# Four PSUM banks for the relation products of a fused graph network kernel, the attribute maximum in the gates' bank, and a constant row brought by a transfer

## Chip, cores and metric

The kernel runs on one core of one Trainium2 chip. The metric is the device time of one execution in microseconds (us). The engines are TensorE (PE; its weight loads are listed apart as PEld), VectorE (DVE), ScalarE (ACT), GpSimd (POOL, called Pool here) and SyncE (SP, which issues transfers). The results of TensorE go to PSUM, which has eight banks of 512 fp32 columns on each of 128 partitions.

## What is computed

A graph with 1250 nodes of 512 features and 20000 edges goes through four layers, each with a residual sum and a layer norm:

```
x = layernorm(x + segment_sum(edge_weight * (x @ W0)[src], dst) + b0)
# the relation layer is applied twice inside the second step (h = relu(first))
def rgcn_gate_layer(x, ...):
    w = einsum('rb,bio->rio', att, basis)            # 2 relations out of 30 bases
    msgs[r] = sigmoid(x_j @ gate_w[r]) * x_j @ w[r]
    return segment_sum(msg of the edge's relation, row) + x @ root + bias
x = layernorm(x + rgcn(relu(rgcn(x))))
x = layernorm(x + gcn(x))                            # weights deg^-1/2, self loop
x = layernorm(x + attention(x, att_bias = edge_attr))  # 8 heads, softmax over a node's edges
```

The attention bias of an edge is `edge_attr_8`; the row maximum of the logits is subtracted before `exp`.

## The kernel before

Nodes are cut into NT = 10 tiles of 128 rows. Neighbour sums are dense products with counting matrices (CT for the two relations) held in SBUF, built at the start. Every fp32 operand is split into a high and a low fp16 part, and a product is the three terms of `THREE` (high x high, low x high, high x low). The order of work on each engine is written out by hand, with semaphores between engines; there is no planner.

**Relation stages.** `z_tile(s, k)` on PE (L1856 to L1873) makes for node tile k the products of x with the mixed weights: in stage s = 1 and 2 (the two relation layers) two products a tile, one per relation, each 12 matmuls of 512 columns (L1872); in stage 3 (the graph convolution) one product with a bias term. Product number `zi` counts through all stages and goes to bank `zi % 2`. `z_high` (ScalarE, L1504) copies it, scaled by the sigmoid gate, to the high half of Z; `z_low` (VectorE, L1042) subtracts to get the low half and raises `zl_made`. PE may reuse a bank when `zl_made` has reached `zi - 1`.

**Beside them on VectorE in layer 1**, after the subtractions of tile 5: the maximum of the edge attributes (L1069) and the low half of root1 (`split_low(0)`, L1017, 2048 columns). PE then turns the maxima into a row (L1943, bank 7, after tile 6), VectorE reduces it (L1083), PE spreads it over 125 partitions (L1946, bank 6, after tile 8) and VectorE subtracts it from all attributes (L1088, `bdiff_made`). ScalarE takes the exponential (L1526). In layer 2 VectorE does `split_low(1)` after tile 5. The gates of layer 2 open on ScalarE in two calls (`gates_opened`, L1494).

**After layer 1's products** PE waits for `bdiff_made` (L2015) and does `roots(0)` to `roots(3)` (L1992, 12 matmuls of 384 columns each, banks 4 to 7), then `chunk_sums` (L2008), with the weight mixes of layer 2 between them (`mix`, L1727, fp32). Each mixed weight is copied by ScalarE (L1467), subtracted by VectorE (L1010, inside `matched`) and stored to DRAM in pairs from ScalarE's queue (`mix_stored`, L1402); the buffers of two pairs alternate. The basis blocks (1 MB each) are loaded by SP (L633): the third and fourth of layer 2 when the last product of layer 1 has ended, each later one when a mix has ended. Gate sums of layer 2 (`gates(1, i)`, L1852) use bank 3, the first of them in the sixth chunk. Between the first loads and layer 1, Pool zeroes the bias array in DRAM by 160 transfers (L807, L810).

**Pool's scatter.** From layer 1's end on, Pool adds the edge values into the bias array by 160 indirect transfers (L844), two at a time, 8 to each of 20 batches. Before the last batch it waits for `loops_out` and writes the constant 64 into the row KH[64] of 10240 fp16 elements (L839), which the attention scores need (`kone_made`, waited for before `scores(0)`).

**Up to the scores.** VectorE computes 80 row maxima (`row_max`, L1223). SP, in its order, copies the heads (L737 to L740), sends the first row of maxima, loads Wo, waits for all scatters, issues two bias loads (L752) and only then sends the second row of maxima (L745), which PE waits for before its third group of scores (L2215). VectorE multiplies with the bias in L1260.

Of the kernel before, what the change touches and what calls it, by code (L numbers as in the profile page):

```python
# [13 lines left out]
P = 128  # L14
# [50 lines left out]
def gnn_resnorm(nc, a, out):  # L65
    ctx = ExitStack()
    with ctx:
# [234 lines left out]
        negative = r2[0:DK, o2 + NN // 2 + P:o2 + NN // 2 + P + DK // 2].bitcast(F16)  # L302
        yT = XX[:, NT * D:NT * D + FT * RB].rearrange("p (f n) -> p f n", f=FT)
# [136 lines left out]
        kone_made = sem("kone_made")  # L440
        wo_in = sem("wo_in")
# [115 lines left out]
        def GATHERED(b):  # L557

            return 0 if b < NT else 2

# [49 lines left out]
        def _(sp):  # L610
# [143 lines left out]

            for o_ in range(FT):
                heads_copied(o_)
# [23 lines left out]
        def _(pool):  # L780
# [49 lines left out]
            for n in range(ZE + ZB + 2 * ZA, ZF):  # L830
                zeros(n)
            pool.iota(bramp, [[-1, GC * EC]], base=GC * EC, channel_multiplier=0,
                      allow_small_or_imprecise_dtypes=True).then_inc(bramp_made, 1)

            pool.wait_ge(zero_out, 16 * ZF)
            for b in range(BATCHES):
                if b == BATCHES - 1:
                    pool.wait_ge(loops_out, NT)
                    pool.memset(KH[DK:DK + 1, :, :], MSCALE).then_inc(kone_made, 1)  # L839
# [13 lines left out]
        def _(dve):  # L853
# [182 lines left out]
            def z_low(s, k):  # L1036

                for r in range(ZRELS[s]):
# [3 lines left out]
                    V.scalar_tensor_tensor(Z[:, r, 1, k, :], mm_out(zi % 2, D), scale, Z[:, r, 0, k, :], ALU.mult,  # L1042
# [13 lines left out]
            for k in range(1, NT):  # L1056
# [24 lines left out]
                if k == 7:  # L1081
                    dve.wait_ge(bmt_done, 1)
                    step(V.tensor_reduce(bmax1[0:HEADS, :], mm_out(7, EC, HEADS), AX.X, ALU.max))  # L1083
                    V.tensor_scalar(diag8[0:HEADS, :], ident[0:HEADS, 0:HEADS], bmax1[0:HEADS, :], None,
                                    ALU.mult).then_inc(bdiag_made, 1)
                if k == 9:
                    dve.wait_ge(bmb_done, 1)
                    V.tensor_tensor(attr[0:EC, :, :], attr[0:EC, :, :],  # L1088
                                    PS[0:EC, 6, 0:HEADS].rearrange("p (u h) -> p u h", u=1).broadcast_to(
# [284 lines left out]
        def _(act):  # L1374
# [123 lines left out]
            def z_high(s, k):  # L1498

                for r in range(ZRELS[s]):  # L1500
# [3 lines left out]
                    S.activation(Z[:, r, 0, k, :], mm_out(zi % 2, D), ACT.Copy, scale=scale).then_inc(zh_made, 1)  # L1504
# [204 lines left out]
        def _(pe):  # L1709
# [130 lines left out]
            def gates(layer, i):  # L1840
# [5 lines left out]
                if i == 0 and layer:  # L1846
                    pe.wait_ge(gate_made, 2)
                if i == ZBATCH:
                    pe.wait_ge(gate_made, 2 * layer + 1)
# [6 lines left out]
            def z_tile(s, k):  # L1856
# [5 lines left out]
                for r in range(ZRELS[s]):  # L1862
                    zi = Z0[s] + k * ZRELS[s] + r
                    if zi >= 2:
                        pe.wait_ge(zl_made, zi - 1)
# [5 lines left out]
                    for n, (lhs, rhs) in enumerate(terms):  # L1871
                        ins = T.matmul(mm_out(zi % 2, D), lhs, rhs, start=n == 0, stop=n == len(terms) - 1)  # L1872
# [66 lines left out]
            for k in range(2, NT):  # L1939
                z_tile(1, k)  # L1940
                if k == 6:
                    pe.wait_ge(bmax_made, 1)
                    T.transpose(mm_out(7, EC, HEADS), bmax[0:EC, :], ident[0:EC, 0:EC]).then_inc(bmt_done, 1)  # L1943
                if k == 8:
                    pe.wait_ge(bdiag_made, 1)
                    T.matmul(mm_out(6, HEADS, EC), ones[0:HEADS, 0:EC], diag8[0:HEADS, :], start=True,  # L1946
# [37 lines left out]
            def roots(c):  # L1984
# [3 lines left out]
                if p_:  # L1988
                    pe.wait_ge(h_made, c - FT + 1)
                for n, (p, q) in enumerate(THREE):  # L1990
# [24 lines left out]
            pe.wait_ge(bdiff_made, 1)  # L2015
# [347 lines left out]
```

## Time and profile before

| | |
|---|---|
| median of 3 runs | 1230.68 us (1227.04 to 1235.55) |
| profiled execution | 1232.0 us |
| its span, first to last instruction | 1230.2 us |
| PE busy | 1167.2 us (95%) |
| DVE busy | 847.2 us (69%) |
| ACT busy | 442.4 us (36%) |
| POOL busy | 374.1 us (30%) |
| mean granted TensorE clock | 0.984 |

A busy PE is not a PE at full speed: the granted clock is 1.00 or about half of it, and a row's busy time grows where it is low. All places are given in us from the span's start. In a timeline row the number in brackets is the idle time of that engine just before the row, with what ended it.

### The profile page before, as it was taken

How to read it: one execution, taken by the hardware profiler on the slowest of the kernel's cores; microseconds unless marked ns; L12 is line 12 of the kernel's file. 1: busy time of each engine (PE TensorE's matmuls, PEld its weight loads, DVE VectorE, ACT ScalarE, POOL GpSimd, SP SyncE). 2: the span in 40 equal slices, each digit the busy share in tenths (PEclk: the TensorE clock that was granted, in tenths of full speed). 3: DMA queues.
4: the chain of work that ended last, by engine and by line, in shares of the span. 5: the costliest groups of instructions: out<-in, count | busy, mean ns of one | idle time of the engine just before them, and what ended most of it. 6: DMA issues, size and time to landing. Idle time of an engine off the chain costs nothing.

```text
span 1230.2 us, 21619 instructions
## 1 busy us (share of the span) xinstructions
PE 1167.2 (95%) x8077; PEld 539.9 (44%) x8078; DVE 847.2 (69%) x1333; ACT 442.4 (36%) x600; POOL 374.1 (30%) x340
## 2 busy tenths in 40 slices
PE   6989999999999989999999999999999899999997
PEld 2334444333444433364444444454333465555553
DVE  7577777344442655652378884657999799899897
ACT  1456666322232222212301103135552355445354
POOL 3034441000350224445554564555557100000000
PEclk9999999999999999999999999999999899999999
DMA  9669995987987988661122212113323566565652
GB/s 311 237 200 326 326 331 150 358 350 261 329 283 272 312 316 286 227 210 2 2 40 47 36 19 70 3 2 45 35 34 58 184 232 228 200 221 198 202 186 111
DMA packets 67490, 222.74 MB, mean 181 GB/s; under 512 B 33200, under 2 KB 38064, under 8 KB 50140
## 3 DMA queue, kind: packets, MB, share of 16 engines
q1 hardware_dynamic: 34846, 156.38, 36.0%
q0 software_dynamic: 28208, 53.10, 18.0%
q10 hardware_dynamic: 4350, 12.07, 2.8%
q8 instruction: 60, 0.98, 0.3%
q14 instruction: 26, 0.21, 0.1%
HBM read 199.90 MB, written 59.92 MB: 211 GB/s over the span
## 4 chain that ended last, share of the span: by engine, by line
PE 45%; DVE 11%; issue 6%; DMA 4%; ACT 2%; ACTq 0%; DVEq 0%
PE PS L1920 13%; PE PS L1872 6%; PE PS L2228 4%; PE PS L2008 4%; PE PS L2215 4%; DVE R L1223 4%; DVE R L1260 4%; DMA w_d<-R 3%; PE PS L2097 2%; PE PS L2274 2%; PE PS L1992 2%; PE PS L1727 2%; PE PS L2245 1%; DVE R L1297 1%; PE PS L1837 1%
## 5 line engine op out<-in xcount | busy, mean ns | idle before, releaser
L844 POOL DMA_INDIRECT bias_d<-R x160 | 276.6, 1729 | 310.2 <-DMA bias_d<-R 204.8
L1920 PE MATMUL PS<-R 128*128 128x512 f16 x900 | 206.3, 382 | 0.0
L810 POOL DMA_DIRECT2D bias_d<-bias_d x159 | 82.6, 526 | 267.3 <-PE PS L1920 123.1
L1683 ACT ACTIVATE R<-PS 128x1024 f32<-128x1024 f32 (+1 forms) x100 | 106.3, 1088 | 108.7 <-PE PS L2215 78.6
L1872 PE MATMUL PS<-W,XX 128*128 128x512 f16 x600 | 137.7, 389 | 5.5 <-DVE R L1042 4.6
L1920 PEld LDWEIGHTS PS<-R 128*128 128x128 f16 x900 | 84.3, 98 | 118.7 <-issue 27.6
L1797 PE MATMUL PS<-R,XX 125*128 125x512 f16 (+2 forms) x612 | 123.1, 343 | 5.7 <-DVE R L958 4.4
L1223 DVE CUSTOM_DVE_ANT_0 R<-PS,R 128x1250 f16<-128x1250 f32 x80 | 116.8, 1460 | 5.5 <-PE PS L2151 2.9
L958 DVE TENSOR_SCALAR R<-W 125x1250 f16<-125x1250 f16 x160 | 89.6, 604 | 37.8 <-PE PS L1797 35.4
L2228 PE MATMUL PS<-R 128*32 128x256 f32 (+1 forms) x1600 | 101.4, 388 | 5.2 <-DVE R L1260 5.2
L2215 PE MATMUL PS<-R 128*128 128x256 f16 (+3 forms) x800 | 100.5, 276 | 5.3 <-ACT R L1683 2.1
L1042 DVE SCALAR_TENSOR_TENSOR R<-PS,gate,R 128x512 f16<-128x512 f32 x50 | 37.3, 750 | 91.8 <-ACT R L1504 91.8
L1260 DVE SCALAR_TENSOR_TENSOR R<-R,W 128x512 f32<-128x512 f32 (+1 forms) x136 | 85.9, 674 | 16.6 <-ACT R L1683 14.2
L1872 PEld LDWEIGHTS PS<-W,XX 128*128 128x128 f16 x600 | 58.7, 100 | 78.6 <-issue 14.1
L2008 PE MATMUL PS<-R 128*128 128x384 f16 (+2 forms) x480 | 92.2, 340 | 0.0
L2215 PEld LDWEIGHTS PS<-R 128*128 128x128 f16 (+1 forms) x800 | 75.1, 99 | 36.8 <-issue 20.2
L1797 PEld LDWEIGHTS PS<-R,XX 125*128 x612 | 56.6, 98 | 65.7 <-issue 23.2
L1487 ACT ACTIVATE stat<-stat 128x1 f32<-128x1 f32 x30 | 8.8, 295 | 181.4 <-DVE stat L1030 165.9
L2008 PEld LDWEIGHTS PS<-R 128*128 128x128 f16 x480 | 44.0, 98 | 58.3 <-issue 28.3
L1504 ACT ACTIVATE R<-PS,gate 128x512 f16<-128x512 f32 x50 | 34.3, 687 | 96.8 <-PE PS L1872 96.1
L2228 PEld LDWEIGHTS PS<-R 128*32 128x32 f32 x1600 | 44.7, 108 | 48.0 <-DVE R L1260 13.5
L2097 PE MATMUL PS<-XX,W 128*128 128x512 f16 (+1 forms) x288 | 61.3, 345 | 1.1 <-ACT R L1622 1.1
(242 smaller groups left out, 1470.3 us busy)
## 6 DMA issues: line engine op xcount, KB each, us to landing
bias_d<-bias_d POOLq DMA_DIRECT2D x159, 320.0 KB, 5.4
R<-in_basis_s SPq DMA_DIRECT2D x32, 1024.0 KB, 7.2
W<-in_basis_s SPq DMA_DIRECT2D x28, 1024.0 KB, 6.3
W<-bias_d SPq DMA_DIRECT2D x27, 1024.0 KB, 4.9
XX<-bias_d SPq DMA_DIRECT2D x13, 1024.0 KB, 4.9
R<-key_d SPq DMA_DIRECT2D x20, 500.0 KB
R<-R SPq DMA_DIRECT2D x120, 80.0 KB, 4.9
W<-bias_d SPq DMA_DIRECT2D x7, 904.0 KB, 4.6
```

The source lines that it names most:

```text
L844: pool.indirect_dma_start(bias_d, bass.IndirectOffsetOnAxis(ap=idx[:, c:c + 1], axis=0), attr[:, c, :], None, bounds_check=DUMP + GC * P - ...
L958: V.tensor_scalar(hot[0:EC, FIXED * (j % 2) + m, 0:NODES], iota16[0:EC, 0:NODES], base[0:EC, bass.ds(t4, 1), j], key[0:EC, bass.ds(lo + m, ...
L1223: V.tensor_tensor_reduce(out=junk[:, 0:NODES], in0=PS[:, b0:b0 + 3, :].rearrange("p a b -> p (a b)")[:, 0:NODES], in1=nmask[:, i, 0:NODES] ...
L1260: ins = V.scalar_tensor_tensor(p, p, BIG, b, ALU.min, ALU.mult)
L1683: S.activation(ER[n % 4][:, :, 0:w, :].rearrange("p g r u -> p g u r"), PS[:, 2 * (n % 2):2 * (n % 2) + 2, :].rearrange("p a (e r) -> p a ...
L1797: ins = T.matmul(mm_out(3 * (j % 2) + b, p1 - p0), own[0:EC, bass.ds(c, 1), :, :].rearrange("p c m w -> p (c m w)"), hots(p0, p1), start=f ...
L1872: ins = T.matmul(mm_out(zi % 2, D), lhs, rhs, start=n == 0, stop=n == len(terms) - 1)
L1920: ins = T.matmul(mm_out(SUM_BANK(s, i), D), lhs, rhs, start=n == 0, stop=n == len(terms) - 1)
L2008: ins = T.matmul(mm_out(4 + f, hi - lo), lhs, rhs, start=False, stop=n == len(terms) - 1, skip_group_check=True)
L2097: ins = T.matmul(mm_out(BANK_OF("q", g), hi - lo), W16[:, 1 + which, q, f, o_ * P:(o_ + 1) * P], XT16[:, p, f, lo:hi], start=n == 0 and f ...
L2215: ins = T.matmul(PS[:, 2 * (n % 2) + i // 2, (i % 2) * RB:(i % 2) * RB + w], key[:, h, j * P:(j + 1) * P], query[:, h, cols], start=k == 0 ...
L2228: ins = T.matmul(PS[32 * i:32 * i + 32, 4 + q, e * RB:e * RB + w], VA[:, j, 4 * q + i, 32 * e:32 * e + 32], ER[n % 4][:, i // 2, 0:w, i % ...
```

## The change

Products of stages 1 and 2 rotate over banks 0, 1, 6 and 7 (`ZBANK`; the third and fourth product of stage 1 go to banks 4 and 5), so PE waits for the subtraction of four products back instead of two. Stage 3 keeps banks 0 and 1. Two waits are added where 6 and 7 come into use, and `roots(2)` and `roots(3)` wait for the last two subtractions of layer 1. The two small matmuls of the attribute maximum go to free columns of bank 3, and PE's wait for `bdiff_made` moves from before `roots(0)` to before the first gate of layer 2. Pool fills a block of 128 x 80 values early, and SP sends it to the row KH[64] ahead of the head copies; Pool's memset and wait before the last batch go.

```
+        scale_row = r2[:, o2 + NN // 2 + P + DK // 2:o2 + NN // 2 + P + DK // 2 + HEADS * NN // P // 2].bitcast(F16)
...
+        def ZBANK(s, k, r):
+
+            m = k * ZRELS[s] + r
+            if s == 3:
+                return m % 2
+            return 2 + m if s == 1 and m in (2, 3) else (0, 1, 6, 7)[m % 4]
...
+            sp.wait_ge(scale_row_made, 1)
+            sp.wait_ge(loops_out, NT)
+            sp.dma_start(KH[DK:DK + 1, :, :].rearrange("u h (k n) -> u (h k) n", n=HEADS * NN // P),
+                         scale_row).then_inc(kone_made, 16)
             for o_ in range(FT):
                 heads_copied(o_)
...
+            pool.memset(scale_row, MSCALE).then_inc(scale_row_made, 1)
...
             for b in range(BATCHES):
-                if b == BATCHES - 1:
-                    pool.wait_ge(loops_out, NT)
-                    pool.memset(KH[DK:DK + 1, :, :], MSCALE).then_inc(kone_made, 1)
...
-                    V.scalar_tensor_tensor(Z[:, r, 1, k, :], mm_out(zi % 2, D), scale, Z[:, r, 0, k, :], ALU.mult,
+                    V.scalar_tensor_tensor(Z[:, r, 1, k, :], mm_out(ZBANK(s, k, r), D), scale, Z[:, r, 0, k, :], ALU.mult,
...
-                    step(V.tensor_reduce(bmax1[0:HEADS, :], mm_out(7, EC, HEADS), AX.X, ALU.max))
+                    step(V.tensor_reduce(bmax1[0:HEADS, :], PS[0:HEADS, 3, P:P + EC], AX.X, ALU.max))
...
-                                    PS[0:EC, 6, 0:HEADS].rearrange("p (u h) -> p u h", u=1).broadcast_to(
+                                    PS[0:EC, 3, DK:DK + HEADS].rearrange("p (u h) -> p u h", u=1).broadcast_to(
...
-                    S.activation(Z[:, r, 0, k, :], mm_out(zi % 2, D), ACT.Copy, scale=scale).then_inc(zh_made, 1)
+                    S.activation(Z[:, r, 0, k, :], mm_out(ZBANK(s, k, r), D), ACT.Copy, scale=scale).then_inc(zh_made, 1)
...
                 if i == 0 and layer:
                     pe.wait_ge(gate_made, 2)
+                    pe.wait_ge(bdiff_made, 1)
...
-                    if zi >= 2:
-                        pe.wait_ge(zl_made, zi - 1)
+                    held = 2 if s == 3 else 4
+                    if s == 3 or zi - Z0[s] >= held:
+                        pe.wait_ge(zl_made, zi - held + 1)
+                    if (s, k, r) == (1, 3, 0):
+                        pe.wait_ge(xt_made, NT)
+                    if (s, k, r) == (2, 1, 0):
+                        pe.wait_ge(h_made, CHUNKS)
...
-                        ins = T.matmul(mm_out(zi % 2, D), lhs, rhs, start=n == 0, stop=n == len(terms) - 1)
+                        ins = T.matmul(mm_out(ZBANK(s, k, r), D), lhs, rhs, start=n == 0, stop=n == len(terms) - 1)
...
-                    T.transpose(mm_out(7, EC, HEADS), bmax[0:EC, :], ident[0:EC, 0:EC]).then_inc(bmt_done, 1)
+                    T.transpose(PS[0:HEADS, 3, P:P + EC], bmax[0:EC, :], ident[0:EC, 0:EC]).then_inc(bmt_done, 1)
...
                 if p_:
                     pe.wait_ge(h_made, c - FT + 1)
+                elif f >= 2:
+                    pe.wait_ge(zl_made, Z0[1] + RELS * NT - FT + f + 1)
...
             pe.wait_ge(w16_made, 1)
-            pe.wait_ge(bdiff_made, 1)
             for c in range(FT):
                 roots(c)
...
-            pe.wait_ge(kone_made, 1)
+            pe.wait_ge(kone_made, 16)
```

On PE, at the end of layer 1's products, this stood before (L1946 spreads the maximum, L1872 are the last two products, L1992 the roots, L2008 the first chunk sum):

```order
L1946 MATMUL PS<-R,ones 125x8 [waits bdiag_made]
L1872 MATMUL PS<-W,XX 128x512 [waits zl_made,xt_made]
L1872 MATMUL PS<-W,XX 128x512 x11
L1872 MATMUL PS<-W,XX 128x512 [waits zl_made]
L1872 MATMUL PS<-W,XX 128x512 x11
L1992 MATMUL PS<-XX,W 128x384 [waits bdiff_made,w16_made]
```

In the changed kernel the same place on PE reads so, with lines 17 to 20 higher:

```order
L1964 MATMUL PS<-R,ones 125x8 [waits bdiag_made]
L1890 MATMUL PS<-W,XX 128x512 [waits zl_made,xt_made]
L1890 MATMUL PS<-W,XX 128x512 x11
L1890 MATMUL PS<-W,XX 128x512 [waits zl_made]
L1890 MATMUL PS<-W,XX 128x512 x11
L2012 MATMUL PS<-XX,W 128x384 [waits w16_made]
L2012 MATMUL PS<-XX,W 128x384 x23
L2012 MATMUL PS<-XX,W 128x384 [waits zl_made]
L2012 MATMUL PS<-XX,W 128x384 x11
L2012 MATMUL PS<-XX,W 128x384 [waits zl_made]
```

No matmul moved; the wait for the attribute subtraction left the first root, and the third and fourth root got one each for a relation product's subtraction.

On SP, before the head copies (L673 loads weights, L737 to L740 copy heads), this stood before:

```order
L704 DMA R<-key_d 128x1000 [waits bm_made] x10
L673 DMA R<-in_Wk 128x2048 [waits bsum_done]
L673 DMA R<-in_Wv 128x2048
L737 DMA R<-R 64x2560 [waits qkh_made]
L739 DMA R<-R 64x2560 [waits qkh_made]
```

And now, on SP, with the new transfer at L767:

```order
L714 DMA R<-key_d 128x1000 [waits bm_made] x10
L683 DMA R<-in_Wk 128x2048 [waits bsum_done]
L683 DMA R<-in_Wv 128x2048
L767 DMA R<-R 1x128x80 [waits loops_out,scale_row_made]
L747 DMA R<-R 64x2560 [waits qkh_made]
L749 DMA R<-R 64x2560 [waits qkh_made]
```

The transfer of the key row was put ahead of all head copies.

## Rows read from the trace of the kernel before

**Rows 1.** The page, part 4: share of the last-ending chain by engine.
```profile
PE 45%; DVE 11%; issue 6%; DMA 4%; ACT 2%; ACTq 0%; DVEq 0%
```
**Rows 2.** Waits of PE: who for whom, us in total, times, longest.
```profile
PE PS L1872 <- DVE R L1042: 4.6, 3, 2.3
PE PS L1992 <- DVE R L1088: 3.0, 1, 3.0
```
**Rows 3.** Timeline of PE, 339 to 399: start, us, instruction, count, idle before.
```profile
339.60 26.06 PE L1872 MATMUL PS<-W,XX 128*128 128x512 f16 x120
365.49 0.27 PE L1943 MATMUL PS<-ident,R 125*8 125x125 f32 x1
368.05 12.20 PE L1872 MATMUL PS<-W,XX 128*128 128x512 f16 x48 [2.28 <-DVE R L1042]
380.17 0.38 PE L1946 MATMUL PS<-R,ones 8*125 8x8 f32 x2
380.49 5.35 PE L1872 MATMUL PS<-W,XX 128*128 128x512 f16 x24
388.89 9.45 PE L1992 MATMUL PS<-XX,W 128*128 128x384 f16 x48 [3.05 <-DVE R L1088]
398.18 1.46 PE L2008 MATMUL PS<-R 128*128 128x384 f16 x8
```
**Rows 4.** Timeline of DVE, 361 to 369.
```profile
361.90 2.46 DVE L1069 TENSOR_REDUCE R<-R 125x8 f32<-125x1280 f32 x1
...
364.94 2.29 DVE L1017 TENSOR_TENSOR W<-R,W 128x2048 f16<-128x2048 f32 x1
367.15 1.40 DVE L1042 SCALAR_TENSOR_TENSOR R<-PS,gate,R 128x512 f16<-128x512 f32 x2
```
**Rows 5.** Windows: length, busy PE, PEld, DVE, ACT, POOL, PE clock, DMA share, GB/s.
```profile
368.00:370.00 2.00, 1.95 (x5) 0.73 (x6) 0.56 (x1) 0.00 (x0) 0.00 (x0) 0.51 1.13 319
...
395.00:398.00 3.00, 3.00 (x20) 1.79 (x19) 0.00 (x0) 0.00 (x0) 0.00 (x0) 1.00 0.07 23
```
**Rows 6.** Timeline of PE, 559 to 612 (layer 2's products).
```profile
559.83 0.44 PE L1852 MATMUL PS<-gw,XX 128*128 128x2 f16 x12
562.14 7.03 PE L1872 MATMUL PS<-W,XX 128*128 128x512 f16 x24 [1.87 <-DVE R L1042]
569.00 0.74 PE L1852 MATMUL PS<-gw,XX 128*128 128x2 f16 x24
569.61 26.06 PE L1872 MATMUL PS<-W,XX 128*128 128x512 f16 x120
596.15 15.70 PE L1872 MATMUL PS<-W,XX 128*128 128x512 f16 x72 [0.47 <-DVE R L1042]
```
**Rows 7.** Timeline of ACT at 560.
```profile
560.52 1.27 ACT L1504 ACTIVATE R<-PS,gate 128x512 f16<-128x512 f32 x2
```
**Rows 8.** Chain and timeline of PE at the end of layer 2's mixes.
```profile
445.49 8.37 DMA w_d<-R
...
458.21 5.30 PE L1992 MATMUL PS<-XX,W 128*128 128x512 f16 x12 [1.33 <-ACT R L1535]
```
**Rows 9.** Timeline of POOL: a scatter after layer 1, and those around the memset.
```profile
494.33 3.52 POOL L844 DMA_INDIRECT bias_d<-R  x1 [8.24 <-DVE R L1136]
...
929.28 1.55 POOL L844 DMA_INDIRECT bias_d<-R  x1 [2.15 <-DMA bias_d<-R]
...
932.72 8.63 POOL L839 MEMSET R<- 1x10240 f16 x1
941.51 1.56 POOL L844 DMA_INDIRECT bias_d<-R  x1 [0.17 <-issue]
...
947.05 1.55 POOL L844 DMA_INDIRECT bias_d<-R  x1 [2.12 <-DMA bias_d<-R]
```
**Rows 10.** Timeline of SP's queue before the scores: issues of transfers.
```profile
963.10 0.81 SPq L752 DMA_DIRECT2D W<-bias_d  x2
967.51 0.77 SPq L745 DMA_DIRECT2D R<-R  x1
```

More of the change, by code:

```diff
@@ L302, in gnn_resnorm @@
         negative = r2[0:DK, o2 + NN // 2 + P:o2 + NN // 2 + P + DK // 2].bitcast(F16)
+        scale_row = r2[:, o2 + NN // 2 + P + DK // 2:o2 + NN // 2 + P + DK // 2 + HEADS * NN // P // 2].bitcast(F16)
+        assert o2 + NN // 2 + P + DK // 2 + HEADS * NN // P // 2 <= KEPT
         yT = XX[:, NT * D:NT * D + FT * RB].rearrange("p (f n) -> p f n", f=FT)
@@ L440, in gnn_resnorm @@
         kone_made = sem("kone_made")
+        scale_row_made = sem("scale_row_made")
         wo_in = sem("wo_in")
@@ L1942, in _ @@
                     pe.wait_ge(bmax_made, 1)
-                    T.transpose(mm_out(7, EC, HEADS), bmax[0:EC, :], ident[0:EC, 0:EC]).then_inc(bmt_done, 1)
+                    T.transpose(PS[0:HEADS, 3, P:P + EC], bmax[0:EC, :], ident[0:EC, 0:EC]).then_inc(bmt_done, 1)
                 if k == 8:
                     pe.wait_ge(bdiag_made, 1)
-                    T.matmul(mm_out(6, HEADS, EC), ones[0:HEADS, 0:EC], diag8[0:HEADS, :], start=True,
+                    T.matmul(PS[0:EC, 3, DK:DK + HEADS], ones[0:HEADS, 0:EC], diag8[0:HEADS, :], start=True,
                              stop=True).then_inc(bmb_done, 1)
```

## Prediction

> **What bounds the kernel now.** I read the page's chain first: TensorE carries 45% of the chain that ended last, VectorE 11% [rows 1]. So a microsecond counts only where PE stands still or runs slow. Next comes the list of waits for PE alone, of which I kept the rows whose line the change touches: the relation products (L1872) wait for VectorE 3 times, 4.6 us in all, and the root products (L1992) once, 3.0 us, for the attribute subtraction of L1088 [rows 2]. PE's timeline gives the places: 2.28 us idle before 368.05 and 3.05 before 388.89 in layer 1 [rows 3], 1.87 before 562.14 and 0.47 before 596.15 in layer 2 [rows 6]. Last, VectorE's timeline says why it was late [rows 4], and the clock windows say what a gap costs after it ended [rows 5].
>
> A relation product is 12 matmuls of 512 columns. In steady state 120 of them start at 339.60 and the next instruction at 365.49: 25.89/120 = 0.2157 us each, 2.59 us a product [rows 3]. Its readers, a ScalarE copy and a VectorE subtraction of some 0.7 us each [rows 4, 7], take well under that, so two banks are enough while nothing else stands in VectorE's queue. The stalls are where something does.
>
> **The rotation, layer 1 (A).** Before 365.5 VectorE does the attribute maximum (2.46 us) and the split of root1 (2.29 us), and comes to the next two subtractions only at 367.15 [rows 4]. From 365.49 to 380.17 are 14.68 us, where 48 matmuls at the steady rate are 10.36 and the small transpose some 0.2: 4.1 us lost, 2.28 of them idle and 1.8 a slow start [rows 3]. The granted clock was 0.51 in the 2 us after the gap, the lower of its two levels, 1.2 GHz [rows 5]. With four banks the product that started at 368.05 needs only the subtraction four products back, the last one before the maximum of 361.90; the first product that needs one of the late subtractions would start near 370.8, and they end at 368.6 [rows 4]. All 4.1 us go. Banks 4 and 5 stand in for 6 and 7 once, for products 2 and 3, since the turned x is still there. The two added waits, on that turn and in layer 2 on the last hidden chunk, are for results that come before the products ahead of them have ended: I cost them at nothing, and at 1 us each if that cover failed.
>
> **The wait for the subtraction (B).** The last 24 product matmuls start at 380.49 and could be followed at 380.49 + 24 x 0.2157 = 385.67. The 48 root matmuls of 384 columns start at 388.89, and the chunk sums at 398.18 [rows 3]. At the steady rate scaled by columns, 0.2157 x 384/512 = 0.162 us, the roots are 7.8 us. Without the wait and the slow start the sums would begin at 393.5: 4.7 us earlier. What is late next: roots 2 and 3 use banks 6 and 7, which the last two products now hold, and wait for their subtractions. The last one ends about 1.5 us after its product (a copy and a subtraction), while roots 0 and 1 occupy PE for 3.9 us, so 2.4 us of cover are left. The moved wait stands before the first layer-2 gate, in the sixth chunk, tens of microseconds after the subtraction. The two small matmuls of the maximum cost the same in bank 3.
>
> **The rotation, layer 2 (C).** Twelve gate matmuls start at 559.83 (0.31 us to the next), then 24 product matmuls should take 5.18 us; they end at 569.00, so 9.17 - 5.49 = 3.7 us are lost, 1.87 idle and 1.8 slow [rows 6]. The wait is for VectorE behind ScalarE, whose two copies start only when the gates open, at 560.52 [rows 7]. The split of root2 costs 596.15 - 569.61 - 25.89 = 0.65 us more [rows 6]. Four banks cover both: C = 4.3 us. The third relation stage keeps two banks.
>
> **Does the gain of A and B pass on?** Behind them come the layer-2 mixes, whose stores follow one another: a buffer pair is reused when an earlier store has landed. Late in that stretch a store of 8.37 us stands in the chain, and PE starts its roots only at 458.21, 12 of them in 5.30 us, slow again [rows 8]. I expect the stretch to move as a block, for first mix, first store and basis loads are all released by PE. What does not move is the zeroing of the bias array, still in the DMA queues when two basis loads go out behind the last product. These two would be needed near 395 and 398, some 9 us sooner, and are released only 4 us sooner. Today the engines are already empty at 395 to 398, a DMA share of 0.07 [rows 5], so with the same bytes and an earlier start they should land by 394. Bounds: all 8.8 us pass on, or 3 if loads and stores hold their time; I take the full sum, since every step is released by PE or by the step before. The slow start at 458 may go, or another come: 2.6 us either way.
>
> **The key row.** Pool's memset lasts 8.63 us, and the next scatter starts at 941.51. Scatter pairs otherwise start 5.54 us apart (941.51 to 947.05), so it would have started at 929.28 + 5.54 = 934.8: the chain gets 6.7 us shorter [rows 9]. Is it on the path? The bias load behind it goes out at 963.10, the last row of maxima at 967.51 [rows 10]: Pool leads by 4.4 us, and today the memset costs nothing. But the maxima end 13.1 us earlier after the change, while Pool's chain, which keeps its own pace after the chunk sums, moves only by A + B = 8.8: without the edit its lead would be 0.1 us, and the landing of the bias loads would show. With it the lead is 4.4 + 8.8 + 6.7 - 13.1 = 6.8 us. The new transfer (128 pieces of 160 bytes) leaves SP when the loops are out, ahead of the head copies, and is needed by the first scores, over 100 us later; whether it takes 1 or 20 us is hidden. Behind its wait on SP stand the head copies, which wait for projections that PE itself begins around then. The small memset of its source runs while Pool waits for transfers. Value 0, bounds -1 and +1.
>
> **Sum.** 4.1 + 4.7 + 4.3 = 13.1 us. Against the profiled execution, 1232.0 us (span 1230.2): 1218.9. The median shown, 1230.7, would give 1217.6. I forecast 1218, own range 1214 to 1223: 5.3 of the 13.1 us are slow starts, of which another execution may have fewer. One per cent, 12.3 us, is about what a measurement of this kernel can tell from no change; the forecast is near that edge.
>
> **The rivals.**
> 1. The loads and stores eat part of A and B. For it: the chain before 458.21 runs through a store [rows 8]. Against: PE releases them. Only 3 of the 8.8 pass: 1232.0 - 3 - 4.3 = 1224.7. Chance 0.17.
> 2. Pool's scatter chain does not follow the 8.8, its pace being that of the traffic. Against: at 494.33 it had waited 8.24 us for VectorE's sums, so it is pulled along [rows 9]. Then the bias loads go out at 963.1 - 6.7 = 956.4, 2 us behind the last row of maxima (954.4). Allowing them 5 us or less to land, up to 4 are lost: 1218.9 + 4 = 1223. Chance 0.08.
> 3. VectorE is the late one, and stall A only moves to a later product. It gives back A: 1218.9 + 4.1 = 1223. Against: the 2.2 us of room between 368.6 and 370.8. Chance 0.05.
> 4. Slower: the rotation itself lowers the clock. PE would meet small gaps at each change of bank, and the clock fall for a tile. 24 matmuls took 6.86 us after such a fall (562.14 to 569.00) instead of 5.18 [rows 6]; 1.7 us on 19 tiles is 32 us: 1218.9 + 32 = 1251. From 8 tiles on it turns the sign. Against: today's two banks change just as often, and 120 matmuls run at 0.2157 us without a gap [rows 3]. Chance 0.03.
>
> The fourth has a rule beside it. The Trainium skill, "TensorE: Matmul & The Clock Gate", section "A second HAM failure mode: psum-queue depth-cycling", tells of a kernel of N=512 matmuls that cycled through banks each iteration and whose micro-idles made the clock fall again and again. By it the relation stages would lose time and the change would be slower; the steady stretch of this trace disagrees, and I side with the trace.
>
> **How the numbers follow.** Forecast 0.67, rivals 0.17, 0.08, 0.05 and 0.03. The range, 1212 to 1227, holds the first three rivals and leaves out the fourth; its low end has 2.6 us for one slow start less and some noise of the runs (1227 to 1236 before). Faster by over 1% is below 1218.4, two thirds of the forecast's share by where its centre lies: 0.45. Slower by over 1%: 0.04, rival 4 and a hundredth for the unnamed. Within 1%: 0.51.
>
> **What would show it.** PE's waits should have no row of relation products on VectorE outside stage 3, and none of roots on the attribute subtraction. From the first layer-1 steady product to the first chunk sum (58.6 us, 339.60 to 398.18) 8.8 us should go, and the clock stay at 1.00. Layer 2's products should take 4.3 us less. Pool's last scatter should lead the last row of maxima by more than 4.4 us. I am wrong if roots wait for the last subtractions, if mixes wait for their basis loads, if the store-bound stretch grows by what was gained, or if the gap before the scores grows.

## The result and the profile after

The changed kernel took 1217.81 us (median of 4 runs, 1216.62 to 1219.36), the kernel before 1230.88 us on the same chip (4 runs, 1227.04 to 1235.55). The ratio is 0.9885, 95% interval 0.9837 to 0.9932. The forecast was 1218.0 us. The profiled execution took 1217.02 us, its span was 1215.1 us and its mean granted clock 0.988 (before: 1232.0, 1230.2 and 0.984).

PE's timeline over layer 1's products in the changed kernel, against [rows 3]: start, us, instruction, count, and in brackets idle time before.

```profile
339.45 26.06 PE L1890 MATMUL PS<-W,XX 128*128 128x512 f16 x120
365.34 0.27 PE L1961 MATMUL PS<-ident,R 125*8 125x125 f32 x1
365.45 10.52 PE L1890 MATMUL PS<-W,XX 128*128 128x512 f16 x48
375.91 0.38 PE L1964 MATMUL PS<-R,ones 8*125 8x8 f32 x2
376.22 5.35 PE L1890 MATMUL PS<-W,XX 128*128 128x512 f16 x24
381.41 7.96 PE L2012 MATMUL PS<-XX,W 128*128 128x384 f16 x48
389.21 1.46 PE L2028 MATMUL PS<-R 128*128 128x384 f16 x8
```

No row has a bracket any more. The 48 matmuls after the small transpose take 10.52 us where they took 12.20, the 2.28 us ahead of them are gone, and the roots follow the last product at once. From the first product to the first chunk sum are 389.21 - 339.45 = 49.76 us; they were 58.58. The windows over the stretch where the gap was, against [rows 5]:

```profile
366.00:368.00 2.00, 2.00 (x11) 0.87 (x9) 2.00 (x3) 0.23 (x1) 0.55 (x3) 1.00 1.01 297
368.00:370.00 2.00, 2.00 (x11) 0.88 (x10) 1.17 (x2) 0.69 (x1) 0.00 (x0) 1.00 0.86 277
```

PE is busy in all of both, and the granted clock is 1.00 (2.4 GHz) where it was 0.51. VectorE (the third figure) is still at its maximum and split through the first window; only nobody waits for it. In layer 2, against [rows 6]:

```profile
542.24 5.34 PE L1890 MATMUL PS<-W,XX 128*128 128x512 f16 x24
547.42 0.44 PE L1865 MATMUL PS<-gw,XX 128*128 128x2 f16 x12
547.72 5.34 PE L1890 MATMUL PS<-W,XX 128*128 128x512 f16 x24
552.90 0.74 PE L1865 MATMUL PS<-gw,XX 128*128 128x2 f16 x24
553.51 41.60 PE L1890 MATMUL PS<-W,XX 128*128 128x512 f16 x192
```

The first 24 product matmuls behind the gates start without the 1.87 us gap and take 5.34 us instead of 7.03, and what were pieces of 120 and 72 with a 0.47 us gap is one run of 192 matmuls, at a granted clock of 1.00 (window 553.5 to 595.1). In the list of PE's waits both groups of [rows 2] are gone; of those that touch this part, these are left:

```profile
PE PS L2234 <- DMA R<-R: 3.1, 1, 3.1
PE PS L1974 <- DVE R L1130: 1.6, 2, 1.2
PE PS L2012 <- ACT R L1547: 1.0, 1, 1.0
```

The first is the scores' wait for the last row of maxima, 2.09 us in the kernel before. Around it, the last of Pool's scatters and of ScalarE's value copies, then SP's queue, against [rows 10], and PE:

```profile
944.35 1.55 POOL L856 DMA_INDIRECT bias_d<-R  x1 [0.30 <-issue]
945.54 0.60 ACT L1640 ACTIVATE R<-PS 128x512 f32<-128x512 f32 x1 [3.91 <-issue]
```
```profile
947.43 0.81 SPq L762 DMA_DIRECT2D W<-bias_d  x2
950.79 0.79 SPq L755 DMA_DIRECT2D R<-R  x1
```
```profile
955.21 3.57 PE L2234 MATMUL PS<-R 128*128 128x256 f16 x16 [3.06 <-DMA R<-R]
```

SP sends the bias loads (947.43) when every scatter has landed and the last value copy has ended, and the row of maxima (950.79) behind them. The copy ended at 945.54 + 0.60 = 946.14, so here the scatters were the last to come: the loads left 1.29 us after the copy and 3.08 us after the last scatter had started. Before, these two intervals were 0.24 and 3.00 us. "Lead" below is the time from the loads' leaving to the row's.

The page's chain by engine answers to [rows 1]:

```profile
PE 70%; DVE 11%; issue 7%; DMA 6%; ACT 5%; ACTq 0%; SPq 0%; DVEq 0%
```

PE's share rose from 45% to 70%; what had carried the rest of the chain stood elsewhere or beside PE, so I take the gain from stages, not from this line. Cut at fixed instructions, us from start to start. M runs from the first chunk sum to layer 2's products (the mixes and their stores), C from there to the first output tile, T on to the third group of scores:

| kernel | A+B | M | C | T | rest |
|---|---|---|---|---|---|
| before | 58.58 | 156.47 | 57.03 | 359.28 | 259.24 |
| after | 49.76 | 153.03 | 52.70 | 360.27 | 259.89 |

So A+B gave 8.8 us, C 4.3 us, M 3.4 us, and T and the rest took back 1.6 us. The first two are the forecast's own terms, to a tenth. The other two nobody had forecast. All stages together make this pair of traces differ by 15.0 us, where the medians differ by 13.1. The experiments had to say whether 13.1 us is what the change is worth, or what this pair of traces shows.

### The profile page after: what moved, and what is told of

The parts are those of the page before. It is cut to its first block, busy times and chain, and to the rows that moved or that the text cites. A ratio compares the mean times of both kernels' runs of the same rounds, so it can differ in the third digit from the quotient of the medians.

```text
span 1215.1 us, 21618 instructions
## 1 busy us (share of the span) xinstructions
PE 1160.9 (96%) x8077; PEld 538.1 (44%) x8078; DVE 846.8 (70%) x1333; ACT 442.3 (36%) x600; POOL 359.4 (30%) x340
## 4 chain that ended last, share of the span: by engine, by line
PE 70%; DVE 11%; issue 7%; DMA 6%; ACT 5%; ACTq 0%; SPq 0%; DVEq 0%
PE PS L1938 17%; PE PS L1890 11%; PE PS L1809 6%; PE PS L2028 5%; PE PS L2247 4%; PE PS L2234 4%; PE PS L1739 4%; DVE R L1235 4%; DVE R L1272 4%; ACT R L1461 4%; PE PS L1757 3%; PE PS L1793 2%; PE PS L2116 2%; PE PS L2293 2%; DMA w_d<-R 2%
## 5 line engine op out<-in xcount | busy, mean ns | idle before, releaser
L856 POOL DMA_INDIRECT bias_d<-R x160 | 270.9, 1693 | 308.5 <-DMA bias_d<-R 224.1
L1890 PE MATMUL PS<-W,XX 128*128 128x512 f16 x600 | 134.2, 383 | 1.2 <-DMA W<-w_d 1.2
```

The costliest lines, as they stand in the source:

```text
L856: pool.indirect_dma_start(bias_d, bass.IndirectOffsetOnAxis(ap=idx[:, c:c + 1], axis=0), attr[:, c, :], None, bounds_check=DUMP + GC * P - ...
L1890: ins = T.matmul(mm_out(ZBANK(s, k, r), D), lhs, rhs, start=n == 0, stop=n == len(terms) - 1)
```

## The experiments

The theory: the change is worth its three stalls (A 4.1, B 4.7, C 4.3 us), each an idle gap and a slow start. The rivals: M's 3.4 us belong to the change; the key row is what keeps the scores from waiting; one of the stalls was worth nothing. Each kernel ran beside the kernel before; batches had different chips, and the median of before was 1227.2 to 1232.9 us in them, so ratios carry the comparison; the 95% intervals of these ratios reach from 2 to 6 us to either side.

**The changed kernel again.** No edit.

> The changed kernel once more, nothing edited, for a tighter ratio and a second trace. Theory (the three terms 4.1 + 4.7 + 4.3 = 13.1 us): ratio near 0.9893, time 1217 to 1218.5. The first trace showed 3.3 us more than that before the second layer's products and a slow start less; if that is part of the change, the trace again has no slow start near 448 and the roots of the fifth chunk start about 9.8 us sooner than the 458.21 of before. Rival: it is chance, and the slow start shows again in some trace.

Measured: 1217.11 us (6 runs, 1212.97 to 1219.62) against 1227.18 (21 runs); ratio 0.9914, 0.9892 to 0.9935. The ratio stands for 10.6 us, with an interval of 8.0 to 13.3; the medians differ by 10.1. The profiled execution has A+B and C again at 49.76 and 52.70 us, but M at 149.68, 3.4 us less than the trace above, with the same program. Near 448 there is again no slow start (the roots of the fifth chunk start at 444.61 and 12 of them take 2.75 us), but the kernel with the memset back, below, shows one there with the same A+B (12 in 5.19 us at 447.12). So that slow start comes and goes by itself, as the rival had it.

**Two banks again**, the rest of the change left as it is. The last product then sits in the bank in which the first mix begins, so the fourth root alone waits for it.

```diff
-            m = k * ZRELS[s] + r
-            if s == 3:
-                return m % 2
-            return 2 + m if s == 1 and m in (2, 3) else (0, 1, 6, 7)[m % 4]
+            return (k * ZRELS[s] + r) % 2
...
-                    held = 2 if s == 3 else 4
-                    if s == 3 or zi - Z0[s] >= held:
-                        pe.wait_ge(zl_made, zi - held + 1)
-                    if (s, k, r) == (1, 3, 0):
-                        pe.wait_ge(xt_made, NT)
-                    if (s, k, r) == (2, 1, 0):
-                        pe.wait_ge(h_made, CHUNKS)
+                    if zi >= 2:
+                        pe.wait_ge(zl_made, zi - 1)
...
-                elif f >= 2:
-                    pe.wait_ge(zl_made, Z0[1] + RELS * NT - FT + f + 1)
+                elif f == 3:
+                    pe.wait_ge(zl_made, Z0[1] + RELS * NT)
```

> Rotation undone in both relation layers, the wait of the roots and the key row as changed. Theory: A and C come back, 4.1 + 4.3 = 8.4 us, so 1226.2 against 1217.8; PE waits 3 times for the subtraction again, 2.3, 1.9 and 0.5 us, with two slow starts. Rival (rotation is worth nothing by itself, the stall only moves): within 1.5 us of 1217.8.

Measured: 1223.78 us (8 runs), ratio 0.997, 0.9953 to 0.9986: 6.7 us behind the changed kernel where 8.4 were expected. PE's timeline of this kernel at the three places, in the fastest of the eight executions (1220.08 us), shows what can be missing:

```profile
367.46 10.52 PE L1882 MATMUL PS<-W,XX 128*128 128x512 f16 x48 [2.29 <-DVE R L1051]
...
551.52 5.34 PE L1882 MATMUL PS<-W,XX 128*128 128x512 f16 x24 [1.87 <-DVE R L1051]
...
583.84 15.70 PE L1882 MATMUL PS<-W,XX 128*128 128x512 f16 x72 [0.47 <-DVE R L1051]
```

The gaps are back to a hundredth (2.29, 1.87, 0.47 us against 2.28, 1.87, 0.47), but the work behind them runs at full rate: 10.52 us where [rows 3] has 12.20, 5.34 where [rows 6] has 7.03. A+B is 52.21 us, 2.45 over the changed kernel, and C 55.34, 2.64 over it. The gap belongs to the program; the slow start behind it comes in one execution and not in another.

**The attribute wait back before the first root.**

```diff
-                    pe.wait_ge(bdiff_made, 1)
...
+            pe.wait_ge(bdiff_made, 1)
             for c in range(FT):
                 roots(c)
```

> The wait for the attribute subtraction put back before the first root, all else as changed. Theory: B comes back, 4.7 us (3.0 idle and 1.7 slow start): 1222.5. If the store-bound stretch behind it absorbs the delay, less: within 2 us of 1217.8. If the lost slow start near 448 depends on it, up to 8 us more: 1225.8.

Measured: 1222.57 us (10 runs), ratio 0.9954, 0.9935 to 0.9973: 5.5 us behind the changed kernel. On PE:

```profile
385.44 9.47 PE L2011 MATMUL PS<-XX,W 128*128 128x384 f16 x48 [3.05 <-DVE R L1100]
```

The same 3.05 us as in [rows 3], and 9.47 - 7.96 = 1.5 us of slow start; A+B is 54.48, 4.72 us over the changed kernel. B is confirmed in place and size.

**Pool's memset back, no transfer.**

```diff
-            sp.dma_start(KH[DK:DK + 1, :, :].rearrange("u h (k n) -> u (h k) n", n=HEADS * NN // P),
-                         scale_row).then_inc(kone_made, 16)
...
-            pool.memset(scale_row, MSCALE).then_inc(scale_row_made, 1)
...
+                if b == BATCHES - 1:
+                    pool.wait_ge(loops_out, NT)
+                    pool.memset(KH[DK:DK + 1, :, :], MSCALE).then_inc(kone_made, 1)
...
-            pe.wait_ge(kone_made, 16)
+            pe.wait_ge(kone_made, 1)
```

> Pool's memset of the key row and its wait put back before the last batch, no transfer, all else as changed. Theory: Pool's chain ends 6.7 us later, so the bias loads go out at 954.1 instead of 947.4, 3.3 us behind the maxima, and the last row of maxima, which stands behind them in SP's queue, lands 3.3 to 4 us later: 1221.5, PE's wait before the scores 3.1 us growing to 6.5 or more. Rival (the memset is hidden as it was before): 1217.8.

Measured: 1217.87 us (4 runs, 1215.85 to 1222.31), ratio 0.9929, 0.9901 to 0.9956. The expected loss did not show. The timelines of POOL, ACT and SP, in order of time:

```profile
911.22 8.62 POOL L849 MEMSET R<- 1x10240 f16 x1
...
938.62 1.55 POOL L854 DMA_INDIRECT bias_d<-R  x1 [0.30 <-issue]
...
946.60 0.60 ACT L1638 ACTIVATE R<-PS 128x512 f32<-128x512 f32 x1 [3.91 <-PE PS L2146]
...
947.23 0.81 SPq L762 DMA_DIRECT2D W<-bias_d  x2
```

Pool's last scatter is out at 938.62, and yet the bias loads leave only at 947.23: 0.03 us after the end of ScalarE's last value copy (946.60 + 0.60). They wait for whichever is later, scatters or copy, and here it is the copy. From the last scatter's start to the loads are 8.61 us, where 3.0 to 3.1 us are enough when the scatters are the late ones, so this trace had some 5.6 us of cover with the memset in it. The changed kernel's first trace had none without it (944.35 and 947.43). Pool's chain simply came out earlier in this execution, and this is the only trace with one memset.

**The key row alone**, on the kernel before: only the key row's lines of the change (its block, transfer and memset; PE's wait for 16).

> The kernel before with the key row's edit alone (small memset early, transfer from SP, none on Pool before the last batch). Theory: in the traces the bias loads leave SP when both the last scatter and the last value copy are done, and these two were 0.2 us apart in the kernel before, so a shorter Pool chain gains nothing: ratio 1.00 within 0.3%. Rival: the memset was on the path, up to 6.7 us gained, ratio 0.995.

Measured: 1226.53 us (10 runs), ratio 0.9978, 0.995 to 1.0005; no difference that can be told: the interval reaches from 6 us gained to 0.6 us lost. In its trace the last scatter starts at 949.13, the last value copy ends at 957.10 and the loads leave at 957.12: the scatters had 5 us of cover and only the copy held the loads, as the theory says. The trace is also a further one of an unrotated kernel: gap A with no slow start, gaps B and C with one.

**Three banks** instead of four (0, 1 and 6).

```diff
-            return 2 + m if s == 1 and m in (2, 3) else (0, 1, 6, 7)[m % 4]
+            return 4 if s == 1 and m == 2 else (0, 1, 6)[m % 3]
...
-                    held = 2 if s == 3 else 4
+                    held = 2 if s == 3 else 3
...
-                    if (s, k, r) == (1, 3, 0):
+                    if (s, k, r) == (1, 2, 1):
...
-                    pe.wait_ge(zl_made, Z0[1] + RELS * NT - FT + f + 1)
+                    pe.wait_ge(zl_made, Z0[1] + RELS * NT - 2 * (f == 2))
```

> The changed kernel with three banks (0, 1, 6) in place of four. Theory: the product that would need one of the two late subtractions starts at about 368.2 in layer 1 and they have ended at 367.8 (first of them), in layer 2 at 562.7 against 562, so PE waits 0.3 us at most: time as changed, 1217.1 within 1.5 us, no wait of products in stages 1 and 2 above 0.5 us. Rival (the depth of four is what hides it): at least 3 us slower and a wait in the trace.

Measured: 1215.7 us (5 runs, 1210.5 to 1217.54), ratio 0.9892, 0.9842 to 0.9942. PE's rows, with no bracket at any of the three places:

```profile
361.33 10.52 PE L1890 MATMUL PS<-W,XX 128*128 128x512 f16 x48
...
542.47 5.34 PE L1890 MATMUL PS<-W,XX 128*128 128x512 f16 x24
...
548.25 41.60 PE L1890 MATMUL PS<-W,XX 128*128 128x512 f16 x192
```

The third bank does all of it; the fourth is spare.

**Four banks in layer 1 only.**

```diff
-            if s == 3:
+            if s >= 2:
                 return m % 2
...
-                    held = 2 if s == 3 else 4
-                    if s == 3 or zi - Z0[s] >= held:
+                    held = 4 if s == 1 else 2
+                    if s > 1 or zi >= held:
...
-                    if (s, k, r) == (2, 1, 0):
-                        pe.wait_ge(h_made, CHUNKS)
```

> Four banks in layer 1 only, two in layer 2. Theory: C comes back: idle 1.87 + 0.5 us always and a slow start of 1.8 us in part of the executions: 2.4 to 4.3 us more than 1217.1, so about 1220.5. The run with no rotation lost 6.7 us in all, so the two layers should share it about evenly. Rival (the stall of layer 2 is absorbed later): 1217.1.

Measured: 1220.04 us (10 runs), ratio 0.9939, 0.9911 to 0.9966: 2.9 us behind the changed kernel's repeat by medians, which is a comparison across batches (3.1 by ratios); against the three banks of its own batch it is 4.3. In this trace the gap stands, again without its slow start:

```profile
549.47 5.34 PE L1888 MATMUL PS<-W,XX 128*128 128x512 f16 x24 [1.87 <-DVE R L1054]
...
581.78 15.70 PE L1888 MATMUL PS<-W,XX 128*128 128x512 f16 x72 [0.48 <-DVE R L1054]
```

C is 55.35 us, 2.65 over the changed kernel; before, with the slow start, it was 4.33 over it.

**The kernel before again.** No edit, one execution.

> The kernel before, unedited, for a second trace of it. Theory: the three idle gaps (2.3, 3.05, 1.87 us) are there again to 0.1 us, while the slow starts behind them come and go from one execution to the next (5.3 us in the first trace). Rival: the slow starts are fixed to the gaps and show all three again with 1.7 to 1.8 us each.

Measured: 1228.84 us, span 1227.1.

```profile
368.44 10.52 PE L1872 MATMUL PS<-W,XX 128*128 128x512 f16 x48 [2.29 <-DVE R L1042]
...
387.60 9.64 PE L1992 MATMUL PS<-XX,W 128*128 128x384 f16 x48 [3.05 <-DVE R L1088]
...
559.20 7.00 PE L1872 MATMUL PS<-W,XX 128*128 128x512 f16 x24 [1.87 <-DVE R L1042]
```

This settles the slow starts: the same program as in [rows 3], and gap A has none here. The granted clock in the 2 us behind gap A is 1.00 here (window 368.5 to 370.5) and was 0.51 in the first trace [rows 5]. Over all traces with a gap: A (2.29 us) was followed by one in 1 of 4, B (3.05 us) in 4 of 4, C (1.87 us) in 3 of 5, the 0.47 us gap in none. Each costs 1.5 to 1.7 us. These are small counts: they show that the slow start is not fixed, and its odds only roughly.

**Three memsets**, one after another, in the kernel with the memset back: the chain of Pool is lengthened until it must show.

```diff
+                    pool.wait_ge(kone_made, 1)
+                    pool.memset(KH[DK:DK + 1, :, :], MSCALE).then_inc(kone_made, 1)
+                    pool.wait_ge(kone_made, 2)
+                    pool.memset(KH[DK:DK + 1, :, :], MSCALE).then_inc(kone_made, 1)
...
-            pe.wait_ge(kone_made, 1)
+            pe.wait_ge(kone_made, 3)
```

> Pool's memset back before the last batch and done three times, one after the other, all else as changed. Theory (Pool's chain has a slack of some 5 to 12 us that differs between executions, as one memset cost nothing): three put 26 us, less the 2 us wait they fill, into the chain, so 24 less the slack: 12 to 19 us slower, 1229 to 1236, with SP's bias loads leaving more than 8 us behind the maxima. Rival (Pool's chain has nothing to do with the end): 1217.9 as with one.

Measured: 1233.73 us (10 runs, 1222.43 to 1240.85), ratio 1.0032, 0.9994 to 1.007: 15.9 us over the single memset by medians, 12.6 by ratios (they ran in different batches).

```profile
964.94 1.55 POOL L858 DMA_INDIRECT bias_d<-R  x1 [0.30 <-issue]
...
967.97 0.81 SPq L762 DMA_DIRECT2D W<-bias_d  x2
...
975.75 3.57 PE L2236 MATMUL PS<-R 128*128 128x256 f16 x16 [25.46 <-DMA R<-R]
```

Here the scatters are the late ones: the loads leave behind the last of them, and PE stands 25.46 us. Two memsets more are 2 x 8.62 = 17.2 us and cost 12.6 to 15.9, so with one memset 1 to 5 us of cover are left on average, an estimate from two batches. The single traces say how uneven that is. Of the nine traces of kernels with the changed wait or banks and no memset, seven have the scatters last: the loads leave 3.0 to 3.1 us after the last scatter has started and 0.5 to 1.3 us after the last copy has ended (the changed kernel and its repeat among them). In the other two, two banks and the held load below, the copy is last and the scatters have 5 us of cover. So Pool's chain is at the edge of the path in this kernel even without the memset, and a trace decides for its own execution only.

**The last row of maxima from ScalarE's queue.** The changed kernel's only new loss is PE's wait for this row. If SP's queue with the bias loads in it was what held it, another queue frees it.

```diff
-            max_row(1)
...
+                if n == 0:
+                    act.wait_ge(mx_made, 2)
+                    act.dma_start(QL[DK:DK + 1, 4:8, :].rearrange("u h (k n) -> u (h k) n", n=P),
+                                  mxT[0:NT * 4, 1, :]).then_inc(mrow_in[1], 16)
```

> The changed kernel with the last row of maxima sent from ScalarE's queue, between its first two exponentials, in place of SP's queue behind two bias loads of 1 MB. In the traces so far PE waits 1.6 to 3.1 us for that row, longest where the bias loads left SP the shortest time before it (lead 3.4 us: 3.06; lead 4.6: 1.6 to 2.05). Theory (the row stands behind the bias loads in one queue, which the changed kernel sharpened): the wait falls below 1 us, 1215.3 against 1217.1. Rival (the landing is limited by the engines' total traffic, whatever the queue): wait and time stay, 1217.1.

Measured: 1218.75 us (9 runs), ratio 0.9919, 0.9894 to 0.9945, and the wait grew. SP, ScalarE's queue and PE:

```profile
947.50 0.43 SPq L762 DMA_DIRECT2D XX<-bias_d  x1
...
950.72 0.85 ACTq L1699 DMA_DIRECT2D R<-R  x1
...
956.83 3.57 PE L2237 MATMUL PS<-R 128*128 128x256 f16 x16 [4.76 <-DMA R<-R]
```

The run tested two things at once: with the row gone from SP, its third bias load (into XX) went out early too, ahead of the row. So it was repeated with that load held back.

**The same, third load held** by `sp.wait_ge(mrow_in[1], 16)` ahead of `load_bias(2)`.

> As the run with the row on ScalarE's queue, but SP holds the third bias load back until the row has landed. In that run the third load left SP at 947.5, before the row at 950.7, and three loads were in flight: the wait grew to 4.76 us. Theory (traffic, not the queue, sets the row's landing): with two loads in flight the wait is that of the changed kernel at the same lead, 2 to 3 us, time 1217 to 1218. Rival (the place in SP's queue sets it): wait below 1 us, 1215.3.

Measured: 1217.61 us (4 runs), ratio 0.9893, 0.9849 to 0.9938.

```profile
955.92 3.57 PE L2238 MATMUL PS<-R 128*128 128x256 f16 x16 [1.71 <-DMA R<-R]
```

1.71 us looks better than 3.06, but here the loads left 4.63 us before the row. The traces with the row on SP behind two loads go roughly by that lead: 3.36 us gives a wait of 3.06 (the changed kernel), 3.69 gives 2.60 (the attribute wait back), 3.91 gives 2.40 (four banks in layer 1 only), 4.01 gives 2.23 (the repeat), 4.12 gives 2.51 (three banks), 4.41 gives 2.09 (the kernel before), and the four with 4.62 or 4.63 give 1.59 to 2.05 us. The 1.71 us from ScalarE's queue at 4.63 lies among these four. With three memsets the row left only 0.85 us behind the loads (968.82 against 967.97), and its matmuls started 6.93 us later, where that was 4.42 us in the changed kernel and 3.11 with two banks. So the queue made no difference that shows; how much of the two loads is still in flight when the row is sent fits all these traces. That the bytes in flight are the cause is a reading of them, which the next run tests.

**The row between the first and second load**, on SP.

```diff
-            for t in range(2):
-                load_bias(t)
+            load_bias(0)
             max_row(1)
+            load_bias(1)
```

> The changed kernel with the row sent by SP between the first and the second bias load, so that only 1 MB is ahead of it. Theory (the bytes in flight before the row set its landing): the row lands within 2 us of its issue, PE's wait falls from 2.2 to 3.1 us to about 1, the second load lands near 955.5 instead of 955 and costs nothing or 0.5 us: 1216 against 1217.1, the best version so far if it holds. Rival (the second load is what the weights then wait for): same or up to 2 us slower, with VectorE waiting over 2 us for the bias before its second weighting.

Measured: 1218.56 us (6 runs), ratio 0.9885, 0.9849 to 0.9921.

```profile
951.26 0.33 SPq L762 DMA_DIRECT2D W<-bias_d  x1
954.68 0.79 SPq L755 DMA_DIRECT2D R<-R  x1
956.96 3.57 PE L2234 MATMUL PS<-R 128*128 128x256 f16 x16 [0.91 <-DMA R<-R]
...
960.57 1.29 DVE L1272 SCALAR_TENSOR_TENSOR R<-R,W 128x512 f32<-128x512 f32 x2 [3.06 <-DMA W<-bias_d]
```

PE's wait falls to 0.91 us, and VectorE waits 3.06 us for the second load instead. The row's matmuls start 2.28 us after the row is sent, with one load ahead of it. The wait was moved, not removed. No version clearly beats the changed kernel; three banks do as well with one bank less.

## Why the prediction was right, and where it was not

**A and B, layer 1: right.** 8.8 us forecast, 58.58 - 49.76 = 8.82 measured. The 2.2 us of room for which rival 3 was refused held, and the roots did not wait for the last two subtractions (48 in 7.96 us, no bracket). Undoing one part at a time gives both back where they were said to be: two banks bring back the 2.29 us, the early attribute wait the 3.05 us.

**C, layer 2: right.** 4.3 us forecast, 57.03 - 52.70 = 4.33 measured, and leaving only layer 2 at two banks costs 2.9 to 4.3 us by medians. The added waits show no idle gap in any trace.

**"Does the gain pass on": right, and M's extra is at least in part chance.** M lasts 149.68 to 155.64 us in the ten traces without the wait ahead of the roots (mean 153.3) and 154.2 to 156.5 us in the four with it (mean 154.9). The changed kernel alone shows 153.03 in one execution and 149.68 in the next, so the 3.4 us of the first pair of traces are within what one program does from run to run. Rival 1 (5.8 of the 8.8 us eaten) falls: no mix waited for its basis load where it was feared, and undoing B costs all of its 4.7 us and not a third. Whether the 1.6 us between the two means hang on the earlier start can't be told from these traces.

**The slow starts: the mis-sized term.** "All 4.1 us go" and C's 3.7 us count a slow start of 1.7 to 1.8 us as if it came every time. It came in the trace of before after all three gaps; behind gap A it came in 1 of 4 traces, behind C in 3 of 5. Sized by these: A 2.45 + 1/4 x 1.7 = 2.9, B 4.8, C 2.65 + 3/5 x 1.7 = 3.7, in all 11.3 us and not 13.1. The forecast named this ("5.3 of the 13.1 us are slow starts, of which another execution may have fewer") but took them whole into its centre.

The slow starts' own part of the 11.3 us is 0.4 + 1.6 + 1.0 = 3.0 us where the forecast had 5.3. The mean granted clock, which is on record for every execution, points the same way without a trace: it was 0.9875 over the 21 executions of the kernel before and 0.9897 over the 6 of the repeat, and 0.0022 of 1220 us are 2.7 us less lost to the lower clock; three banks against the 19 executions beside it give 0.9894 - 0.9869, 3.1 us. Across the other runs with all three gaps gone this difference is 1.7 us in one batch and 4.9 and 6.3 in the last, so the forecast's 5.3 is not excluded; and the mean clock counts every slow stretch of the execution, not these three alone. The medians can't decide between 11.3 and 13.1: the repeat's ratio says 10.6 us, 8.0 to 13.3, and three banks, alike in all stages, 13.3 us by a ratio of 0.9892.

That the first result, 13.07 us by medians of 4 runs each, agrees with the forecast's sum to a tenth is luck: its interval reaches from 8.4 to 20 us, and in its traces M's 3.4 us stand beside the three terms.

**The key row: no gain to be told, as forecast; the lead was forecast wrongly.** The forecast has it at "Value 0, bounds -1 and +1". The kernel with its edit alone came to a ratio of 0.9978, between 6 us gained and 0.6 us lost; putting the memset back moved the ratio from 0.9914 to 0.9929, within the noise. Both lean to a gain of 2 us, and neither shows one. The step that failed is "With it the lead is 4.4 + 8.8 + 6.7 - 13.1 = 6.8 us": it measured 950.79 - 947.43 = 3.36 us, less than before. Two things were left out of it. The first is that SP waits for the last value copy as well as for the scatters. That copy moves with PE and ended 4.65 us before the row of maxima left, before (962.86 and 967.51) and after (946.14 and 950.79), so that no edit on Pool could have made the lead longer than 4.63 us. It was 4.41 before, and taking the memset away had some 0.2 us to give in that trace. The second is M: the loads left where they were expected (947.6), but the maxima came 16.7 us sooner than before and not 13.1, by M's 3.4 us. So the lead of "more than 4.4 us", which was to show the forecast right, did not come by the measure that gave 4.4, and one of the signs of being wrong did show in the first trace: "if the gap before the scores grows". It grew from 2.09 to 3.06 us, which costs 1 us. Rival 2 had the right worry (bias loads at 956.4); they left at 947.43.

The other step, "without the edit its lead would be 0.1 us, and the landing of the bias loads would show", is not borne out by the one trace with the memset back: no loss, and the scatters early. It took the chain's pace as fixed, and that is loose by itself: its 17th scatter started at 495.74, 499.75, 497.86, 502.93 and 483.07 us in five traces of kernels that are alike up to there but for a few microseconds on PE. With an early chain the memset is hidden; with a late one, as in the changed kernel's first trace, where the scatters were the last to come without it, the 6.7 us of the memset would have stood in the path. How often it would count stays open: the 4 runs with one memset have an interval of 0.9901 to 0.9956, whose upper end would allow a loss of some 5 us.

**Rival 4, the rotation lowers the clock: refuted.** 192 matmuls through four banks took 41.60 us, 0.2167 us each, at a granted clock of 1.00, as with two banks (120 in 26.06). The rule of the Trainium skill in "TensorE: Matmul & The Clock Gate", section "A second HAM failure mode: psum-queue depth-cycling", would have made the relation stages slower; this kernel shows nothing of it, with three banks or four.

**What stays open.** T and the rest are together 617.9 to 618.5 us in the three traces with all waits of before. In the changed kernel and its repeat they are 620.2 and 619.9, 620.6 with the attribute wait back, 619.1 with one memset, 618.9 with three banks, 618.8 with two, 621.9 with the row on ScalarE's queue; but 618.6, 618.5 and 618.4 us, as before, with four banks in layer 1 only, with the third load held and with the row between the loads. A later landing of the row is 1 us of it in the first trace, and the scatters that come last explain that landing; for the remainder no row was found, and between 0 and 2 us of the gain may be lost there. It stays open as well what sets the pace of Pool's chain in one execution, and why it came early with the memset back.

## What to carry to other kernels

Take a stall in two parts: the gap, which recurs to a hundredth of a microsecond and can be counted whole, and the slow start behind it, which one trace shows or doesn't. Count the slow start by how often it comes. Take a second trace of the kernel before, and compare the mean granted clock over all executions of both kernels. Where readers of a rotating buffer are quick but stand behind other work in their queue, one buffer more than they need when they are on time may already be enough, as it was here. Ahead of saying that an edit on a side chain will count, list everything its consumer waits for, with the time at which each comes in the new schedule: the others bound what the edit can give.

## What the runs showed that I had not expected

- The same short idle gap lets the granted clock fall to its lower level in one execution and not in another. In these traces 1.87 us did so 3 times in 5, 2.29 us once in 4, 3.05 us each time in 4, 0.47 us never.
- A small transfer that goes out a few microseconds behind large loads lands later the more of them are in flight: PE's wait was 1.6 to 3.1 us behind two loads that had left 3.4 to 4.6 us before, 4.76 behind three, 0.91 behind one. Whose queue it took made no difference that shows (1.71 us from ScalarE's, 1.59 to 2.05 from SP's, at the same lead).
- A chain of indirect scatters beside heavy traffic keeps no fixed pace: from the first to the last of the 160 scatters it took 537.8 to 544.0 us in nine traces of the changed kernel and its variants without a memset, and 537.0 us in the one that had a memset of 8.62 us in the chain.
